# Routed experts in 256-row blocks with copied stationary weights, and the residual plus normalised x formed in place on ScalarE

## The chip, the cores and the metric

One core of a Trainium2 chip runs the kernel. The metric is the device time of one execution in microseconds (us). The engines are TensorE (PE in the profile; its weight loads are PEld), VectorE (DVE), ScalarE (ACT), GpSimd (POOL) and SyncE (SP). Each runs its own stream of instructions, and they meet only at semaphores.

## The reference

x has 8 x 1024 tokens of 256 features, so 8192 tokens. The layer is a macaron: half a feed-forward step, one attention step, half a feed-forward step, all in float32.

```python
x = x + 0.5 * ffn(layernorm(x))
x = x + attn(layernorm(x))
x = x + 0.5 * ffn(layernorm(x))

def attn(x):                       # per batch of 1024 tokens, D = 256
    q, k, v = x @ Wq.T, x @ Wk.T, x @ Wv.T
    fk = rfft(k); fk = fk / (abs(fk) + 1e-8)
    fq = rfft(q); fq = fq / (abs(fq) + 1e-8)
    return x + irfft(cumsum(fk * rfft(v), axis=-2) * conj(fq))

def ffn(x):
    shared = (silu(x @ sw1) * (x @ sw3)) @ sw2          # hidden 512
    s = sigmoid(x @ router_w.T)                         # 8 experts
    # the top 2 of s + bias, with gates s / sum(s of the two)
    routed = sum over the token's 2 experts: gate_e * (gelu(x @ ew1[e]) @ ew2[e])   # hidden 256
    return shared + routed
```

attn is given layernorm(x) and adds it once more, so the attention step yields x + layernorm(x) + values.

## The kernel before

Tokens are handled in tiles of 128 and chunks of J = 4 tiles (512 tokens, CH = 16 chunks). All of x stays in SBUF as X. Five stages follow each other: phase A and phase B of the first feed-forward, attention, phase A and phase B of the second, then a last loop that combines and stores. Within a stage every engine runs the same loop of steps (`run_steps`, L106: a few steps written out, then a hardware loop of 2 or 4 steps a turn, then the rest) in an order written by hand. No planner is involved. A step mixes work of neighbouring items, so that each engine has something to do while the others finish.

Every matmul operand is split in a high and a low part ("h" and "l", fp32r), and each product is three matmuls (`three`, L645; its lines L647 to L649 are what the profile shows). ScalarE makes the high part with a copy (L476) and VectorE the low part with a subtraction (`low`, L906, shown as L908).

Phase A computes the shared feed-forward and the router, and scatters each token's normalised row (264 floats, with the row's goal in column 256) into DRAM lists, one per expert, by GpSimd's indirect DMAs (L401). Then `block_table` (L1081) counts on one partition how many 128-row blocks each expert has, and writes a table of BLOCKS = 136 entries with the first row of each block and its expert. SP fills up the last block of each expert (eight DMAs at L322, each with a register read from the table by `value_load`).

Phase B walks over the blocks two at a time: PAIRS = 68 steps a layer. For pair s:

- SP reads two registers and loads two blocks of 128 rows into XB, a ring of 4 slots (L328). It waits for s_bl of the pair 4 before.
- PE transposes them (four 128 x 128 transposes, L783), ScalarE makes XBT high, VectorE first copies the goal column (L1128) and then makes XBT low.
- PE computes the hidden layer with the token block as stationary operand (128 x 128) and the expert's weights as moving operand, 256 columns, at an address from a register: 2 blocks x 2 k x 3 = 12 matmuls. ScalarE applies Gelu (L561), with tokens on the partitions.
- PE transposes the result (four again, L773), ScalarE makes HT high from PSUM, VectorE HT low.
- PE computes the output, again 12 matmuls of 256 columns. VectorE copies it to YB (L1134), and GpSimd scatters it to DRAM with two indirect DMAs (L412), at rows given by `goal`.

PE's order in step s (L766) is: transposes of hidden s-1, transposes of input s+1, 12 matmuls of hidden s, two register loads for s+1, 12 matmuls of output s-1. ScalarE's is HT high s-1, XBT high s+1, Gelu s. VectorE's is HT low s-1, goal and XBT low s+1, YB s-1.

In attention (16 steps) VectorE's step (L1138) adds the values of chunk s-3 to X (L1146), combines the two experts' results of chunk s+2 with X (L1155), takes its statistics (L915, L919), and then does the products of the spectra (L1170 to L1205). GpSimd's step (L423) has the sums of squares (L428), the prefix sums (L440 to L450), rstd and shift (L374, `rstd_of`), the products L456 to L462, and last X = X + XN for chunk s+1 (L466). ScalarE's step (L566) evicts PSUM, has the inverse square root by tables (L589 to L595), and makes XN = x * rstd + shift with four activations (L601), before it evicts q (L610) and the high part of the transposed XN (L614).

## Time and profile before

| | us |
|---|---|
| median of 3 runs | 1908.54 (1908.44 to 1914.2) |
| the profiled execution, its own time | 1914.37 |
| its span, first to last instruction | 1912.5 |
| PE busy | 1524.1 (80%) |
| PEld busy | 1354.9 (71%) |
| DVE busy | 1297.0 (68%) |
| ACT busy | 740.8 (39%) |
| POOL busy | 850.9 (44%) |

The profile is of one execution. The shares are means over stages with different limits, so they have to be read stage by stage. Matmuls overlap each other: the duration shown for one (some 280 ns) is longer than the distance from one to the next.

### The profile page before, as it was taken

How to read it: one execution, taken by the hardware profiler on the slowest of the kernel's cores; microseconds unless marked ns; L12 is line 12 of the kernel's file. 1: busy time of each engine (PE TensorE's matmuls, PEld its weight loads, DVE VectorE, ACT ScalarE, POOL GpSimd, SP SyncE). 2: the span in 40 equal slices, each digit the busy share in tenths (PEclk: the TensorE clock that was granted, in tenths of full speed). 3: DMA queues.
4: the chain of work that ended last, by engine and by line, in shares of the span. 5: the costliest groups of instructions: out<-in, count | busy, mean ns of one | idle time of the engine just before them, and what ended most of it. 6: DMA issues, size and time to landing. Idle time of an engine off the chain costs nothing. (4 is left out here: it accounts for less than half of the span.)

```text
span 1912.5 us, 35484 instructions
## 1 busy us (share of the span) xinstructions
PE 1524.1 (80%) x10030; PEld 1354.9 (71%) x10031; DVE 1297.0 (68%) x3148; ACT 740.8 (39%) x1161; POOL 850.9 (44%) x948
## 2 busy tenths in 40 slices
PE   2899999939999965777777874999999849999930
PEld 1777777739999965677777763777777749999930
DVE  4777888734555536899999855778887635555557
ACT  4333343314444423555555533343333224444410
POOL 1444444404444432666666642544545314444420
PEclk9999999969999986899999986999999979999975
DMA  8211111124444432111111001111111134444469
GB/s 286 88 52 51 55 47 45 57 63 127 133 134 134 128 125 66 45 44 44 44 44 44 0 1 48 55 46 45 52 50 54 49 85 133 133 134 133 131 212 348
DMA packets 123780, 170.36 MB, mean 89 GB/s; under 512 B 14880, under 2 KB 105392, under 8 KB 123440
## 3 DMA queue, kind: packets, MB, share of 16 engines
q1 hardware_dynamic: 89936, 91.05, 16.2%
q0 software_dynamic: 25344, 70.29, 10.1%
q10 hardware_dynamic: 8448, 8.39, 1.3%
q8 instruction: 25, 0.41, 0.1%
q14 instruction: 27, 0.22, 0.0%
HBM read 91.03 MB, written 81.89 MB: 90 GB/s over the span
## 5 line engine op out<-in xcount | busy, mean ns | idle before, releaser
L412 POOL DMA_INDIRECT results<-b_yb,b_goal x272 | 261.5, 961 | 368.0 <-DVE b_yb L1134 296.3
L401 POOL DMA_INDIRECT lists<-a_rows,a_slots x256 | 265.3, 1036 | 117.5 <-issue 64.5
L1134 DVE COPY b_yb<-bank 128x512 f32<-128x512 f32 x136 | 94.1, 692 | 195.8 <-PE bank L649 183.5
L647 PE MATMUL bank<-a_sw2h,a_uh 128*128 128x256 f32 x512 | 152.2, 297 | 37.5 <-DVE a_xtl L908 30.5
L476 ACT ACTIVATE a_uh<-a_gate_u 128x512 fp32r<-128x512 f32 x128 | 77.1, 624 | 255.0 <-PE bank L649 202.1
L476 ACT ACTIVATE b_hth<-bank 128x512 fp32r<-128x512 f32 x136 | 81.5, 599 | 242.9 <-PE bank L773 239.7
L647 PE MATMUL bank<-ew_h,b_hth 128*128 x544 | 162.8, 299 | 15.9 <-DVE b_htl L908 7.7
L647 PE MATMUL bank<-t_wfh,t_xah 128*128 128x256 f32 x384 | 126.2, 329 | 57.9 <-DVE t_xal L908 57.9
L647 PE MATMUL bank<-ew_h,b_xbth 128*128 x544 | 166.3, 306 | 0.6 <-DVE b_xbtl L908 0.4
L648 PE MATMUL bank<-ew_l,b_xbth 128*128 x544 | 154.8, 284 | 0.0
L649 PE MATMUL bank<-ew_h,b_xbtl 128*128 x544 | 154.6, 284 | 0.0
L649 PE MATMUL bank<-ew_h,b_htl 128*128 x544 | 153.7, 283 | 0.0
L648 PE MATMUL bank<-ew_l,b_hth 128*128 x544 | 153.6, 282 | 0.0
L648 PE MATMUL bank<-a_sw2l,a_uh 128*128 128x256 f32 x512 | 146.3, 286 | 0.0
L649 PE MATMUL bank<-a_sw2h,a_ul 128*128 128x256 f32 x512 | 146.1, 285 | 0.0
L908 DVE TENSOR_TENSOR b_htl<-bank,b_hth 128x512 fp32r<-128x512 f32 x136 | 94.1, 692 | 57.4 <-ACT b_hth L476 49.9
L647 PEld LDWEIGHTS bank<-t_wfh,t_xah 128*128 128x128 f32 x384 | 85.2, 222 | 64.5 <-DVE t_xal L908 32.1
L647 PEld LDWEIGHTS bank<-a_sw2h,a_uh 128*128 128x128 f32 x512 | 98.6, 193 | 44.2 <-DVE a_xtl L908 36.2
L783 PE MATMUL bank<-cst,b_xb 128*128 128x128 f32 x544 | 84.1, 278 | 52.9 <-DMA b_xb<-lists 27.7
L647 PEld LDWEIGHTS bank<-ew_h,b_hth 128*128 128x128 f32 x544 | 103.4, 190 | 32.0 <-issue 30.9
L396 POOL COPY a_rows<-tok 128x4 int32 (+1 forms) x64 | 12.8, 200 | 250.3 <-DVE a_slots L1024 199.3
L648 PE MATMUL bank<-t_wfl,t_xah 128*128 128x256 f32 x384 | 119.8, 312 | 0.0
(190 smaller groups left out, 4776.9 us busy)
## 6 DMA issues: line engine op xcount, KB each, us to landing
b_xb<-lists SPq DMA_DIRECT2D x272, 132.0 KB
t_yg<-results SPq DMA_DIRECT2D x32, 512.0 KB, 4.7
f_yf<-results SPq DMA_DIRECT2D x32, 512.0 KB, 10.8
X<-in_L_attn_x SPq DMA_DIRECT2D x16, 512.0 KB, 4.1
out<-X ACTq DMA_DIRECT2D x16, 512.0 KB, 7.2
results<-b_yb,b_goal POOLq DMA_INDIRECT x272
w_raw_ew<-in_L_ffn_ew SPq DMA_DIRECT2D x2, 2048.0 KB, 12.6
lists<-a_rows,a_slots POOLq DMA_INDIRECT x256
```

What stands on the lines that cost most here:

```text
L396: ch.link(pool.tensor_copy(rows[:, q, :, D:D + 1].bitcast(I32), tok[:, bass.ds(c * J + k * TILES, J)].unsqueeze(2)))
L401: pool.indirect_dma_start(out=lists, out_offset=bass.IndirectOffsetOnAxis(ap=slots[:, q, k, j:j + 1], axis=0), in_=rows[:, q, j, :], in_of ...
L412: pool.indirect_dma_start(out=results, out_offset=bass.IndirectOffsetOnAxis(ap=goal[:, slot, blk:blk + 1], axis=0), in_=YB[:, slot, blk, : ...
L476: return act.activation(o, i, ACT.Copy)
L647: pe.matmul(o, a("h"), b("h"), start=first, stop=False)
L648: pe.matmul(o, a("h"), b("l"), start=False, stop=False)
L649: return pe.matmul(o, a("l"), b("h"), start=False, stop=last)
L783: ins = pe.transpose(bank[:, 1 - par, (2 * k + blk) * P:(2 * k + blk + 1) * P], XB[:, slot, blk, k * P:(k + 1) * P], ident)
L908: return dve.tensor_tensor(o, v, h.bitcast(F32), ALU.subtract)
L1134: dve.tensor_copy(YB[:, slot].rearrange("p b d -> p (b d)"), bank[:, 7 - par, :]).then_inc(s_yok, 1)
```

## The change

A block has BR = 256 rows, and an expert's list is filled up to a multiple of 256. A step of phase B now is one block of one expert. The number of steps a layer is the most that can be needed, PAIRS = (16384 + 8 * 255) // 256 = 71. The hidden layer is computed with the weights as stationary operand, copied before by ScalarE (high) and VectorE (low) from the expert's place to a double buffer W1, and with the 256 tokens as moving operand, so that the hidden features lie on the partitions and HB needs no transpose. HT is made from HB in SBUF. `goal` is copied last in VectorE's step, with a semaphore of its own that SP waits for. In attention, GpSimd makes rstd_1 = 1 + rstd, and ScalarE forms X = X * rstd_1 + shift in place with four more activations, in place of GpSimd's addition. The diff, cut to its core:

```diff
@@ block_table: TILES -> FULL = TOKENS // BR, BLOCKS -> PAIRS, P -> BR throughout; CAP = TOKENS + BR; SPARE = E * BR
+PAIRS = (TOPK * TOKENS + E * (BR - 1)) // BR
+TURNS = [(PAIRS - i + 3) // 4 for i in range(4)]
+        HB = place("b", "hb", [P, 2, 2 * HR], F32)
+        HT = {h: place("b", f"ht{h}", [P, 2, KD, BR], F32R) for h in "hl"}
+        W1 = {h: place("b", f"w1{h}", [P, 2, KD * HR], F32R) for h in "hl"}
@@ sync
-            sp.dma_start(lists[E * CAP:E * CAP + E * P, :], fill[E * P:2 * E * P, :]).then_inc(s_spare, 16)
+            sp.dma_start(lists[E * CAP:E * CAP + SPARE, :], fill[SPARE:2 * SPARE, :]).then_inc(s_spare, 16)
-                    sp.dma_start(lists[bass.ds(end, P), :], fill[e * P:(e + 1) * P, :]).then_inc(s_tail, 16)
+                    sp.dma_start(lists[bass.ds(end, BR), :], fill[e * BR:(e + 1) * BR, :]).then_inc(s_tail, 16)
-                    atleast(sp, s_bl, n + (p0 - 3) if not isinstance(n, int) or n >= 4 else 0)
-                    for blk in range(2):
-                        row = sp.value_load(table[0:1, bass.ds(n * 2 + blk, 1)], ...)
-                        sp.dma_start(XB[:, slot, blk, :], lists[bass.ds(row, P), :]).then_inc(s_xb[slot], 16)
+                    atleast(sp, s_goal, n + (p0 - 3) if not isinstance(n, int) or n >= 4 else 0)
+                    row = sp.value_load(table[0:1, bass.ds(n, 1)], min_val=0, max_val=E * CAP + SPARE - BR)
+                    sp.dma_start(XB[:, slot, :, :],
+                                 lists[bass.ds(row, BR), :].rearrange("(b p) r -> p b r", p=P)).then_inc(s_xb[slot], 16)
@@ gpsimd
+                if residual:
+                    apart(pool)
+                    ch.link(pool.tensor_scalar(rstd_1[:, q, :], rstd[:, q, :], 1.0, 1.0, ALU.add, ALU.mult))
+                    ch.settle()
-                if nxt:
-                    pool.wait_ge(s_txn, s + 2)
-                    xc = X[:, bass.ds((s + 1) * J, J), :]
-                    pool.tensor_tensor(xc, xc, XN[:], ALU.add).then_inc(s_add, 1)
@@ scalar, phase_b
-                    if inside(s - 1, PAIRS):
-                        act.wait_ge(s_hT, s + p0)
-                        copy(HT["h"][:, 1 - par]..., bank[:, 4 + 1 - par, :]).then_inc(s_hh, 1)
                     if inside(s + 1, PAIRS):
                         ...
+                        e = act.value_load(table[0:1, bass.ds(s + (PAIRS + 1), 1)], min_val=0, max_val=E - 1)
+                        atleast(act, s_mm1, s + p0)
+                        copy(W1["h"][:, 1 - par], EW[1, "h"]...[:, bass.ds(e, 1), :]...).then_inc(s_w1h, 1)
                     if inside(s, PAIRS):
                         act.wait_ge(s_mm1, s + (p0 + 1))
+                        atleast(act, s_hl, s + (p0 - 1))
                         act.activation(HB[:, par], bank[:, 2 + par, :], ACT.Gelu).then_inc(s_gelu, 1)
+                        act.wait_ge(s_gelu, s + (p0 + 1))
+                        atleast(act, s_yps, s + (p0 - 1))
+                        copy(HT["h"][:, par].rearrange("p m t -> p (m t)"), HB[:, par]).then_inc(s_hh, 1)
@@ scalar, attention
-                    atleast(act, s_add, s + 1)
                     atleast(act, s_atp, s + 1)
                     for j in range(J):
                         ins = act.activation(XN[:, j, :], ...)
                     ins.then_inc(s_txn, 1)
+                    act.wait_ge(s_txn, s + 2)
+                    apart(act)
+                    for j in range(J):
+                        xt = X[:, bass.ds((s + 1) * J + j, 1), :].rearrange("p a d -> p (a d)")
+                        ins = act.activation(xt, xt, ACT.Identity, bias=shift[:, 1 - par, j:j + 1],
+                                             scale=rstd_1[:, 1 - par, j:j + 1])
+                    ins.then_inc(s_add, 1)
@@ tensor, phase_b
-                    for blk in range(2):
-                        pe.reg_load(offset[par][blk], table[0:1, bass.ds(s * 2 + (BLOCKS + blk), 1)])
+                    pe.reg_load(offset[par], table[0:1, bass.ds(s + PAIRS, 1)])
-                    if inside(s - 1, PAIRS):
-                        pe.wait_ge(s_gelu, s + p0)
-                        ...                      # the transposes of HB, L771 to L775
+                        pe.wait_ge(s_w1h, s + (p0 + 1))
+                        pe.wait_ge(s_w1l, s + (p0 + 1))
                         atleast(pe, s_gelu, s + (p0 - 1))
-                        for blk in range(2):
+                        for m in range(KD):
                             for k in range(KD):
-                                ins = three(bank[:, 2 + par, blk * HR:(blk + 1) * HR],
-                                            lambda h: XBT[h][:, par, k, blk, :],
-                                            lambda h: expert(1, h, at[blk], k), k == 0, k == KD - 1)
+                                ins = three(bank[:, 2 + par, m * BR:(m + 1) * BR],
+                                            lambda h: W1[h][:, par, k * HR + m * P:k * HR + (m + 1) * P],
+                                            lambda h: XBT[h][:, par, k].rearrange("p b t -> p (b t)"),
+                                            k == 0, k == KD - 1)
@@ vector, phase_b, the whole step after
+                    if inside(s + 1, PAIRS):
+                        dve.wait_ge(s_bh, s + (p0 + 2))
+                        low(XBT["l"][:, 1 - par]...).then_inc(s_bl, 1)
+                        e = dve.value_load(table[0:1, bass.ds(s + (PAIRS + 1), 1)], min_val=0, max_val=E - 1)
+                        atleast(dve, s_mm1, s + p0)
+                        dve.tensor_copy(W1["l"][:, 1 - par], EW[1, "l"]...[:, bass.ds(e, 1), :]...).then_inc(s_w1l, 1)
+                    if inside(s, PAIRS):
+                        dve.wait_ge(s_hh, s + (p0 + 1))
+                        low(HT["l"][:, par]..., HB[:, par], HT["h"][:, par]...).then_inc(s_hl, 1)
+                    if inside(s - 1, PAIRS):
+                        dve.wait_ge(s_yps, s + p0)
+                        dve.tensor_copy(YB[:, slot]..., bank[:, 7 - par, :]).then_inc(s_yok, 1)
+                    if inside(s + 1, PAIRS):
+                        atleast(dve, s_ysc[slot], turn * 32 + YW[slot] * layer)
+                        dve.tensor_copy(goal[:, slot, :], XB[:, slot, :, D].bitcast(I32)).then_inc(s_goal, 1)
```

The loops of phase B end three steps earlier (`PAIRS - 3`), and three steps are written out behind them, because 71 is no multiple of 4.

## Rows read from the trace of the kernel before

**Rows 1.** Phase B, attention: window, length, busy PE, PEld, DVE, ACT, POOL, clock, DMA.
```profile
421.00:705.00 284.00, 269.78 (x2176) 260.72 (x2176) 142.46 (x272) 116.13 (x205) 130.72 (x136) 0.98 0.42 126
723.00:1112.00 389.00, 292.75 (x1814) 272.38 (x1815) 341.74 (x478) 214.70 (x237) 242.00 (x212) 0.89 0.13 41
```
**Rows 2.** PE timeline, first and last input transposes of a phase B (start, us).
```profile
421.40 1.09 PE L783 MATMUL bank<-cst,b_xb 128*128 128x128 f32 x4 [25.72 <-DMA b_xb<-lists]
...
690.47 0.60 PE L783 MATMUL bank<-cst,b_xb 128*128 128x128 f32 x4
...
1556.46 1.08 PE L783 MATMUL bank<-cst,b_xb 128*128 128x128 f32 x4 [25.18 <-issue]
...
1823.54 0.60 PE L783 MATMUL bank<-cst,b_xb 128*128 128x128 f32 x4
```
**Rows 3.** PE timeline, one step of phase B and the next one's transposes.
```profile
541.81 0.60 PE L773 MATMUL bank<-cst,b_hb 128*128 128x128 f32 x4
542.25 0.60 PE L783 MATMUL bank<-cst,b_xb 128*128 128x128 f32 x4
...
545.56 0.60 PE L773 MATMUL bank<-cst,b_hb 128*128 128x128 f32 x4
```
**Rows 4.** ACT and DVE groups over the whole kernel: count, busy, mean ns, idle before.
```profile
L908 DVE TENSOR_TENSOR b_htl<-bank,b_hth 128x512 fp32r<-128x512 f32 x136 | 94.1, 692 | 57.4 <-ACT b_hth L476 49.9
L1128 DVE COPY b_goal<-b_xb x136: 157/169/410, 423.2 to 1825.2; 128x2 int32<-128x2 int32 x136
L476 ACT ACTIVATE a_uh<-a_gate_u 128x512 fp32r<-128x512 f32 x128 | 77.1, 624 | 255.0 <-PE bank L649 202.1
```
**Rows 5.** POOL timeline, the first scatter of two consecutive steps of phase B.
```profile
455.74 0.96 POOL L412 DMA_INDIRECT results<-b_yb,b_goal  x1 [2.10 <-DVE b_yb L1134]
...
459.02 0.96 POOL L412 DMA_INDIRECT results<-b_yb,b_goal  x1 [1.06 <-issue]
```
**Rows 6.** SP timeline: issues without and with a register read.
```profile
706.97 0.46 SPq L345 DMA_DIRECT2D t_raw_w<-in_L_attn_Wv  x1
...
405.31 10.09 SPq L322 DMA_DIRECT2D lists<-in_c_fill  x8
...
9.55 5.52 SPq L309 DMA_DIRECT2D lists<-in_c_fill  x1
```
**Rows 7.** DVE timeline: the largest operation of the block table, the first statistics.
```profile
400.83 2.41 DVE L1103 TENSOR_REDUCE b_line<-b_past 1x272 f32<-1x2176 f32 x1
...
26.59 1.41 DVE L915 BATCH_NORM_STATS2 st<-X 128x6 f32<-128x256 f32 x4 [0.18 <-DVE carry L1077]
```
**Rows 8.** DVE timeline, one step of attention.
```profile
952.78 1.21 DVE L908 TENSOR_TENSOR t_xal<-bank,t_xah 128x1024 fp32r<-128x1024 f32 x1
956.41 1.60 DVE L1203 TENSOR_TENSOR t_kv<-t_kv 128x508 f32<-128x508 f32 x1
958.05 0.69 DVE L1205 TENSOR_TENSOR t_kv<-t_ta,t_tb 128x508 f32<-128x508 f32 x1
967.82 0.66 DVE L1170 TENSOR_TENSOR t_ta<-bank,t_fq 128x508 f32<-128x508 f32 x1
976.85 1.21 DVE L908 TENSOR_TENSOR t_xal<-bank,t_xah 128x1024 fp32r<-128x1024 f32 x1
...
L1170 DVE TENSOR_TENSOR t_ta<-bank,t_fq 128x508 f32<-128x508 f32 x16 | 10.7, 668 | 31.5 <-PE bank L865 31.5
```
**Rows 9.** POOL, PE and ACT timelines of the same step.
```profile
953.86 2.38 POOL L466 TENSOR_TENSOR X<-X,t_xn 128x1024 f32 x1
956.20 1.26 POOL L428 TENSOR_TENSOR t_sq<-t_sq 128x508 f32<-128x508 f32 x1
...
966.64 0.59 PE L865 MATMUL bank<-t_px,cst 128*128 128x256 f32 x2
...
967.41 2.08 ACT L601 ACTIVATE t_xn<-X,shift,rstd 128x256 f32 x4
971.07 1.02 ACT L476 ACTIVATE t_xah<-bank 128x1024 fp32r<-128x1024 f32 x1
```

More of the change, by code:

```diff
@@ L160, in build @@
         shift = sb("shift", [P, 2, J], F32)
+        rstd_1 = sb("rstd_1", [P, 2, J], F32)
         neg_one = sb("neg_one", [P, J], F32)
@@ L805, in step @@
                         for blk in range(2):
-                            for k in range(KD):
+                            for m in range(KD):
                                 ins = three(bank[:, 7 - par, blk * D:(blk + 1) * D],
-                                            lambda h: HT[h][:, 1 - par, k, blk, :],
-                                            lambda h: expert(2, h, at[blk], k), k == 0, k == KD - 1)
+                                            lambda h: HT[h][:, 1 - par, m, blk * P:(blk + 1) * P],
+                                            lambda h: expert(2, h, before, m * HR, HR), m == 0, m == KD - 1)
                         ins.then_inc(s_yps, 1)
                 pe.wait_ge(s_table, layer + 1)
-                offset = [[pe.alloc_register(f"expert_{layer}_{par}_{blk}") for blk in range(2)] for par in range(2)]
-                run_steps(pe, step, -1, 4, PAIRS - 4, PAIRS + 1, 4)
+                offset = [pe.alloc_register(f"expert_{layer}_{par}") for par in range(2)]
+                run_steps(pe, step, -1, 4, PAIRS - 3, PAIRS + 1, 4)
             def attention_weights():
@@ L1114, in phase_b @@
                 p0 = PAIRS * layer
+                dve.wait_ge(s_table, layer + 1)
                 def step(s, u, q):
```

118 lines of the change are left out of this document (52 added, 66 removed).

## The prediction, made before the changed kernel was run

> **What bounds the kernel now.** I read the page's slices first, then the busy time by stage, then the timelines of the stages that the diff touches. A share of the span would mislead: phase B and attention have different limits. In phase B PE is busy 269.78 of 284 us at a clock of 0.98, its weight loads 260.72, while DVE has 142.46, ACT 116.13 and POOL 130.72 [rows 1]. In attention DVE has 341.74 of 389 us and PE 292.75 [rows 1], most of DVE's idle time lying at the stage's two ends and in a few waits for PE.
>
> Phase B's pace is the distance from one step's input transposes to the next one's. From the first to the last of 68 steps are 690.47 - 421.40 = 269.1 us, over 67 intervals 4.02 us; in the second layer 1823.54 - 1556.46 = 267.1 us, 3.99 us [rows 2]. A step in which nothing stalls takes 545.56 - 541.81 = 3.75 us [rows 3]. So PE's own work makes 3.75 us, and stalls make some 0.26 us in the mean.
>
> **Phase B, PE.** The four transposes of the hidden tile go. Four transposes take 542.25 - 541.81 = 0.44 us of PE [rows 3]. Both kernels have 24 matmuls of 256 columns and 4 input transposes beside them. Stationary and moving operand change places in 12 matmuls, for which I take no price: one 128-column load and one 256-column matmul stay one of each. PE's work for a step becomes 3.75 - 0.44 = 3.31 us. One of two register loads a step goes as well. The steps rise from 68 to 71, intervals from 67 to 70, since all 71 are computed whatever the counts are. At 3.31 us they take 231.7 us; at the old mean 4.02 they would take 281.4. The stalls of 0.26 us should shrink. Before, the stalled instruction is mostly the second product, waiting for HT low, whose chain starts with PE's transposes only one product ahead (transpose, ScalarE, VectorE, 1.45 us, of which 0.6 + 0.69 are the two engines [rows 4]). After, the chain is Gelu, HT high, HT low, 0.6 + 0.62 + 0.69 = 1.9 us with some 0.3 us of handing over, 2.2 us, and it has an output product, a set of transposes and a hidden product to hide in, 1.43 + 0.44 + 1.43 = 3.3 us (a product of 12 matmuls being half of what 3.75 - 2 x 0.44 leaves). I leave a third of the stalls, 0.09 us: 3.40 us a step, 70 x 3.40 = 238.0 us. That is -31.1 us in the first layer and -29.1 in the second.
>
> **Phase B, the others, against 3.40 us.** ScalarE gains the copy to W1 high. Its nearest row is the copy between two SBUF tiles of the same size, 0.624 us [rows 4]. Four of them are 2.5 us, and a register read is added. VectorE has XBT low, W1 low, HT low, YB, goal: 0.69 for each of the first four at most, the subtraction HT low being 0.692 [rows 4] and 0.17 for the last, 2.9 us. The copy W1 low shows in no row: it lies between 0.16 us (the smallest goal copy) and 0.69 us (the subtraction of the same size); I take 0.69 as the nearest in size. What the register read costs shows on SP only: an issue takes 0.46 us without one, and 10.09 / 8 = 1.26 us with one, so up to 0.8 us [rows 6]. I count it as hidden on both engines, because it runs in the sequencer while the copy before it (0.6 to 0.69 us) is still at work; if it isn't hidden, VectorE needs 2.9 + 0.8 = 3.7 us, and this is a rival. POOL's least distance between the first scatters of two steps is 459.02 - 455.74 = 3.28 us, where the idle time is put to issue, not to DVE [rows 5]. So POOL can just follow a PE at 3.31. SP has one read and one DMA of twice the rows instead of two of each: less. The ring of four slots is freed later in the step (goal is now last), which leaves some two and a half steps, 8.5 us, for one issue and one transfer of 264 KB, at a DMA share of 0.42 now [rows 1].
>
> The Trainium skill has a rule against this change. "SBUF — State Buffer", section "Who interferes with whom", says that a VectorE copy between SBUF tiles in a two-port mode and a GpSimd instruction exclude each other for their whole length, and that GpSimd's descriptor generation needs that port. What the rows show is the goal copy, between 157 and 410 ns with a median of 169 [rows 4], so a copy was held by 0.24 us at most. By the rule in full, a scatter and W1 low would wait for each other up to 0.96 us a step. The rule's own result, as a mechanism of this kernel, is the second rival.
>
> **Around phase B.** The block table has 71 entries instead of 136 and 32 thresholds instead of 64. Its largest reduction falls from 2.41 us [rows 7] to some 1.3, and the operations ahead of it, which are shorter and shrink alike, by 2.2 us together: -3.3 us a layer. The eight fills carry twice the rows. One fill of 1024 rows is issued in 5.52 us, 5.4 ns a row [rows 6]; 128 rows more are +0.7 us if that holds for them, and nothing if the issue has a fixed price as the loads of 256 rows with 0.46 us suggest. The eight lie between 0 and +5.5; I take +2.8. The first hidden product waits for W1 too, +0.5 us. The sum is 0 a layer, between -3 and +3. At the start SP issues a fill of 2048 rows before the loads of X: +5.5 us for the X loads. The first statistics start at 26.59 with no wait for X [rows 7], so part of it is hidden behind expert weights: +2 us, between 0 and +5.
>
> **Attention.** GpSimd's addition of 2.38 us goes [rows 9]. DVE's L1203 took 1.60 us, and L1205, of the same size and also on SBUF tiles, 0.69 [rows 8]; L1203 ran against GpSimd's L428 (956.20 to 957.46 [rows 9]). With the addition gone, L428 follows 2.38 us earlier, beside products that read PSUM and are not slowed. So DVE gets back 1.60 - 0.69 = 0.9 us a step. What is late next is PE: L1170 needs the prefix sums' last matmul, which starts at 966.64 and ends at 967.1 to 967.2, and L1170 ran at 967.82 [rows 8, 9]. So 0.65 to 0.73 us can be kept. Nine of the steps are of this kind; in the others L1170 waits for PE already (31.5 us in 16 [rows 8]) and nothing is gained. 9 x 0.7 = -6.5 us, between -14 (0.9 us in all 16) and 0. ScalarE's four more activations cost 2.08 us like those of L601 [rows 9]. They stand ahead of q's eviction and of XA high, which then starts at 973.2 instead of 971.07 [rows 9] and ends at 974.2; the subtraction that waits for it starts at 976.85 (a period of 24.07 after 952.78 [rows 8]), and at 976.1 with the gain. Thus they are covered by 1.8 us, and would cost 2.1 us x 16 = 33 us if that cover were gone. GpSimd's rstd_1 comes before s_rstd, a small operation that I put at 0.3 us (the goal copy's 0.17 [rows 4] with a wait behind it); GpSimd is idle 147 of 389 us [rows 1], and what it takes is lost in that.
>
> **The sum** against the profiled execution, 1914.37 us: -31.1 - 29.1 - 6.5 + 0 + 2 = -64.7, so 1849.7 us. That execution is 5.8 us above the median of 1908.54; with the same difference off, 1843.9: I say 1844 us.
>
> **Rivals.**
> - Register reads on the path, VectorE as the bound. For it: VectorE's 2.9 us is the second longest sum, and its order makes every step wait for ScalarE twice. Against it: PE reads two registers a step now, and still has steps of 3.75 us without a gap. At 3.7 us a step, 70 x 3.7 = 259.0: -10.1 - 8.1, and 1914.4 - 18.2 - 6.5 + 2 - 5.8 = 1886 us.
> - The copy and the scatters exclude each other, by 0.33 us a step (half of 0.69, the copy in a mode twice as fast, holding GpSimd once). GpSimd's 3.28 becomes 3.61 us, 252.7 us a layer: -16.4 - 14.4, 1873 us.
> - The slow side: GpSimd is held by a copy of full length, 3.28 + 0.69 = 3.97 us. 70 x 3.97 = 277.9: +8.8 + 10.8, 1914.4 + 19.6 - 6.5 + 2 - 5.8 = 1924 us. It decides from 269.1 / 70 = 3.84 us a step on. For it: GpSimd's floor is so near PE's. Against it: the goal copies, always beside scatters, have a median of 169 ns.
> - Attention turns the other way, ScalarE's activations delaying XA high: up to +33 us, with the gain of phase B left 1883 us. Against it stands ScalarE's idle time, 174 of 389 us [rows 1], 10.9 us a step.
>
> **How the numbers follow.** The forecast has a chance of 0.63, the first rival 0.12, the second 0.11, attention 0.03, the slow one 0.06, and 0.05 is left for a phase B with no stall at all (3.31: 70 x 3.31 = 231.7, -6.3 twice more) together with attention at its best, 1844 - 12.6 - 7.5 = 1824 us. The range is 1822 to 1882: below it nearly nothing, above it the first rival's greater part and the slow one. From 1908.54, 0.3% is 5.7 us, about what a measurement of this kernel can tell from no change. Faster by more has 0.90, within it 0.03, slower by more 0.07.
>
> **What would show it.** Right: in phase B the distance of input transposes near 3.4 us with PE (PEld too) the busiest engine, 71 of them; L1203 at 0.69; DVE still without gaps in attention, period 23.4. Wrong: W1 low followed by idle time of PE on it (first rival); scatters longer than 0.96 us or idle time of POOL's put to a DVE copy, W1 low longer than 0.69 (second and slow rival); t_xal waiting for ACT (attention). The prediction falls if a step of phase B takes more than 3.6 us.

## The result, and the profile after

| group of runs | before, us | after, us | ratio, 95% interval | phase B of after, first and second layer |
|---|---|---|---|---|
| first (the prediction's) | 1908.35 | 1922.89 | 1.0058, 1.0039 to 1.0077 | 271.2, 269.6 |
| c_after, chip 2 | 1910.08 | 1916.40 | 1.0015, 0.9976 to 1.0054 | 274.0, 274.2 |
| z_after, chip 6 | 1876.81 | 1823.30 | 0.9715, 0.9699 to 0.9732 | 231.5, 231.3 |

Forecast were 1844 us and a range of 1822 to 1882: the measured result, 1922.89, lies outside and on the slow side. The later groups show that the sign hangs on the chip, or on its state at the time. Where before takes 1908 to 1910 us (the first group's chip and chip 2; on chip 4, with before at 1908.58, only variants of after ran) the change gives nothing or costs 0.6%; where before takes 1877 (chip 6; on chip 3 again only variants) it gives 53.5 us. Chips 2 and 4 served one group of runs each, so a lasting property of a chip can't be told from a state that it was in. Ratios leave the slow executions out: 1940.72 us among the 20 of after, 3081.38 among the 11 of e_attn, 2595.1 among the three of before beside e_noscatter.

Phase B is one profiled execution's, from the start of the first input transpose to the start of the very last one. That is 0.3 us more than the starts in [rows 2] give; before's two layers, counted so, are 269.4 and 267.4 us.

The two profiled executions of after, the first group's (own time 1905.47, span 1903.6, the fastest of its 20 and 17 us under their median; where the median execution lost those 17 us no trace shows) and z_after's (span 1821.6), have the same instructions. First the windows of [rows 1] (phase B and attention, the same columns), in the first group's:

```profile
421.00:705.00 284.00, 248.11 (x1988) 241.42 (x1986) 168.64 (x355) 170.13 (x285) 143.79 (x141) 0.97 0.44 131
723.00:1112.00 389.00, 295.06 (x1836) 274.46 (x1837) 331.19 (x481) 246.48 (x302) 211.26 (x214) 0.89 0.13 41
```

PE's busy time in phase B has fallen from 269.78 us to 248.11, the part of the forecast that came true; but the window is still filled: 36 us of PE's time are gaps now, against 14. The page's groups (whole kernel; count, busy, mean ns, idle time before and what ended it) say at which instruction:

```profile
L911 DVE TENSOR_TENSOR b_htl<-b_hb,b_hth 128x512 fp32r<-128x512 f32 x142 | 98.3, 692 | 185.8 <-ACT b_hth L480 147.8
L661 PE MATMUL bank<-ew_h,b_hth 128*128 x568 | 166.9, 294 | 56.2 <-DVE b_htl L911 55.5
L661 PE MATMUL bank<-b_xbth,b_w1h 128*128 128x256 f32 x568 | 175.0, 308 | 3.5 <-DVE b_w1l L1130 2.2
L566 ACT ACTIVATE b_hb<-bank 128x512 f32<-128x512 f32 x142 | 83.9, 591 | 112.1 <-remote 86.4
```

PE waits for HT low (55.5 us in both layers), hardly for W1 low (2.2), and Gelu, L566, waits 86.4 us with "remote" as releaser: the profile finds no end of an instruction near the moment at which the wait ended. The same two products in z_after have no such wait:

```profile
L661 PE MATMUL bank<-b_xbth,b_w1h 128*128 128x256 f32 x568 | 173.6, 306 | 3.0 <-DVE b_w1l L1130 3.0
L661 PE MATMUL bank<-ew_h,b_hth 128*128 x568 | 159.5, 281 | 1.5 <-DVE b_htl L911 1.5
```

One slow step out of the first group's trace, PE's transposes, the hidden product's last matmul, Gelu and what follows (start, duration, in brackets the idle time before and its releaser):

```profile
509.23 0.28 PE L663 MATMUL bank<-b_xbth,b_w1l 128*128 128x256 f32 x1
...
510.77 0.60 PE L786 MATMUL bank<-cst,b_xb 128*128 128x128 f32 x4
...
511.60 0.60 ACT L566 ACTIVATE b_hb<-bank 128x512 f32<-128x512 f32 x1 [2.12 <-remote]
512.23 0.63 ACT L480 ACTIVATE b_hth<-b_hb 128x512 fp32r<-128x512 f32 x1
512.89 0.69 DVE L911 TENSOR_TENSOR b_htl<-b_hb,b_hth 128x512 fp32r<-128x512 f32 x1 [2.62 <-ACT b_hth L480]
...
513.82 0.38 PE L661 MATMUL bank<-ew_h,b_hth 128*128 x1 [1.02 <-DVE b_htl L911]
...
515.34 0.60 PE L786 MATMUL bank<-cst,b_xb 128*128 128x128 f32 x4
```

The hidden product's last matmul ends at 509.23 + 0.28 = 509.51. Gelu needs nothing else and sits idle, yet starts at 511.60: PE's release comes 2.1 us after the matmul's modelled end. From there the chain takes just the 2.2 us that the prediction gave it (511.60 to 513.82), but with 2.1 + 2.2 = 4.3 us in front of a cover of 3.3, PE stands idle for 1.02 us, and the step lasts 515.34 - 510.77 = 4.57 us. The step before it took 3.29. So phase B alternates over long stretches: of 70 steps of the first layer some 40 take 3.28 to 3.4 us, 22 take 4.3 to 5.5, two 7.0 and 8.5. In z_after 66 of 70 take 3.28 or 3.29 us, and Gelu starts when the product ends:

```profile
505.45 0.60 ACT L566 ACTIVATE b_hb<-bank 128x512 f32<-128x512 f32 x1
...
506.67 0.60 PE L786 MATMUL bank<-cst,b_xb 128*128 128x128 f32 x4
506.75 0.69 DVE L911 TENSOR_TENSOR b_htl<-b_hb,b_hth 128x512 fp32r<-128x512 f32 x1 [0.81 <-ACT b_hth L480]
...
509.95 0.60 PE L786 MATMUL bank<-cst,b_xb 128*128 128x128 f32 x4
```

How late a release is, is read as the moment at which PE raises the semaphore less the modelled end of the matmul that carries it. In the first group's trace of after it is over 1 us for the hidden product in 36 of the 132 steps whose release is on record, mostly 2.0 to 2.8 (and 0.4 to 0.6 in the step between two such), 1.7 to 1.9 us for the input transposes in some 45 steps and 2.1 to 2.3 for the output product in some 42; the late ones of one stretch come together (513.15, 513.21, 513.34). The kernel before shows the same thing smaller, mostly 0.4 to 0.6 us behind its HT transposes and up to 0.8 behind the output product. In z_after none is over 0.1 us.

Two things go with it. Late releases aren't confined to phase B: in phase A of the first trace of before the release of the shared output product is late by up to 1.3 us, in after's by up to 1.4, in z_after never. And the traces with late releases lack records of semaphores: of 143 rises behind the hidden product after has 136, of 143 behind the output product 127, before 91 of 137 behind the hidden product, though the matmuls' own records are all there; no trace without late releases lacks more than one of such a semaphore. Each timed execution has its span and clock from the profiler, so whether releases come late without the recording no run shows.

### The profile page after: what moved, and what is told of

It reads as the page before. It is cut to its first block and busy times, and to the rows that moved or that the text cites. A ratio compares the mean times of both kernels' runs of the same rounds, so it can differ in the third digit from the quotient of the medians.

```text
span 1903.6 us, 34118 instructions
## 1 busy us (share of the span) xinstructions
PE 1481.1 (78%) x9654; PEld 1318.8 (69%) x9655; DVE 1330.2 (70%) x3315; ACT 878.2 (46%) x1386; POOL 839.8 (44%) x960
## 5 line engine op out<-in xcount | busy, mean ns | idle before, releaser
L420 POOL DMA_INDIRECT results<-b_yb,b_goal x284 | 290.7, 1023 | 336.2 <-DVE b_yb L1139 237.0
L911 DVE TENSOR_TENSOR b_htl<-b_hb,b_hth 128x512 fp32r<-128x512 f32 x142 | 98.3, 692 | 185.8 <-ACT b_hth L480 147.8
L661 PE MATMUL bank<-ew_h,b_hth 128*128 x568 | 166.9, 294 | 56.2 <-DVE b_htl L911 55.5
L661 PE MATMUL bank<-b_xbth,b_w1h 128*128 128x256 f32 x568 | 175.0, 308 | 3.5 <-DVE b_w1l L1130 2.2
L661 PE MATMUL bank<-a_sw2h,a_uh 128*128 128x256 f32 x512 | 151.9, 297 | 23.2 <-DVE a_xtl L911 16.1
L662 PE MATMUL bank<-ew_l,b_hth 128*128 x568 | 163.6, 288 | 0.0
L662 PE MATMUL bank<-b_xbtl,b_w1h 128*128 128x256 f32 x568 | 162.3, 286 | 0.0
L663 PE MATMUL bank<-b_xbth,b_w1l 128*128 128x256 f32 x568 | 161.9, 285 | 0.0
L661 PEld LDWEIGHTS bank<-ew_h,b_hth 128*128 128x128 f32 x568 | 110.3, 194 | 64.7 <-issue 64.7
L480 ACT ACTIVATE b_xbth<-bank 128x512 fp32r<-128x512 f32 x142 | 84.5, 595 | 141.3 <-PE bank L786 125.5
L566 ACT ACTIVATE b_hb<-bank 128x512 f32<-128x512 f32 x142 | 83.9, 591 | 112.1 <-remote 86.4
L496 ACT ACTIVATE a_gate_u<-bank 128x512 f32<-128x512 f32 x128 | 75.4, 589 | 128.2 <-PE bank L663 63.9
L911 DVE TENSOR_TENSOR b_xbtl<-bank,b_xbth 128x512 fp32r<-128x512 f32 x142 | 97.5, 687 | 47.9 <-ACT b_xbth L480 45.0
```

What stands on the lines that cost most here:

```text
L420: pool.indirect_dma_start(out=results, out_offset=bass.IndirectOffsetOnAxis(ap=goal[:, slot, blk:blk + 1], axis=0), in_=YB[:, slot, blk, : ...
L480: return act.activation(o, i, ACT.Copy)
L496: act.activation(gate_u[:, m % 2, :], bank[:, 2 + 2 * (m % 2), :], ACT.Sigmoid).then_inc(s_sig, 1)
L566: act.activation(HB[:, par], bank[:, 2 + par, :], ACT.Gelu).then_inc(s_gelu, 1)
L661: pe.matmul(o, a("h"), b("h"), start=first, stop=False)
L662: pe.matmul(o, a("h"), b("l"), start=False, stop=False)
```

## Experiments

Theory at the start: PE's releases come late by 2 us whatever the kernel does, and the cover is too short for that. Rivals: the W1 copies or register reads disturb PE or the chain; PE's own work is what is late.

### One part alone, more cover, fewer suspects (chip 3)

e_attn is the kernel before with the attention part alone:

```
-                    pool.tensor_tensor(xc, xc, XN[:], ALU.add).then_inc(s_add, 1)
+                        ins = act.activation(xt, xt, ACT.Identity, bias=shift[:, 1 - par, j:j + 1],
+                                             scale=rstd_1[:, 1 - par, j:j + 1])
```

> The kernel before with the attention part alone (blocks of 128 rows as before; rstd_1, the residual in place on ScalarE, GpSimd's addition gone). Theory: the two parts are independent and phase B is where the forecast failed. Then this gives what the attention stage showed in the trace after, 423.4 - 419.5 = 3.9 us, so 1904 to 1905 against 1908.5, with the stage near 419.5 us and phase B unchanged at 269 and 267 us. Rival: the stage gained 3.9 us only in the one profiled execution, and ScalarE's four activations more cost as much as GpSimd's addition: 1908 to 1909. Second rival: ScalarE delays XA high in most steps, 1915 or more.

Measured: 1881.56 against 1877.21, ratio 1.0021 (1.0012 to 1.0031). The part alone doesn't gain, it costs 4 us. Its attention stage, from VectorE's first combination (L1155) to the last matmul of the values, takes 423.1 us. It is 423.4 in the first trace of before, and between 417.6 and 424.2 in the kernels with blocks of 256, whose attention is e_attn's, so a gain of the part isn't clear of the scatter between traces; its phases B take 253.8 and 255.2 us, though their code is that of before (269.4, 267.4). None of its releases is late. The clue to all that follows is in the other column: before itself measured 31 us less here.

e_deep puts the output product two steps behind the hidden one:

```
-                        pe.wait_ge(s_hl, s + p0)
+                        pe.wait_ge(s_hl, s + (p0 - 1))
-                                             lambda h: HT[h][:, 1 - par, m, ...
+                                             lambda h: HT[h][:, (u + 2) % 4, m, ...
```

> The kernel after, with PE's output product two steps behind the hidden product instead of one (four buffers of HT and four expert registers for two, eight rows of goal for four, VectorE waits for the scatter's landing before it fills YB). The chain from the hidden product over Gelu, HT high and HT low has then two whole PE steps, 6.6 us, to hide in, instead of 3.3. Theory: the long steps come from releases by PE that arrive up to 2.0 to 2.8 us after the last matmul's modelled end, so that a chain of 2.2 us becomes 4.3 to 5.0 us against a cover of 3.3. With 6.6 us it is covered: a step of phase B near 3.3 to 3.4 us, 70 x 3.35 = 234.5 instead of 271.2 and 269.6, 72 us less than after: 1835 to 1855 us. Rival: PE's own work is what is late, so the releases tell the truth and the recorded starts run ahead of the work; then PE needs some 3.8 us a step whatever the cover is, and the time stays at 1900 to 1925.

e_nocopy:

```
-                        copy(W1["h"][:, 1 - par], EW[1, "h"] ... [:, bass.ds(e, 1), :] ...
-                                             lambda h: W1[h][:, par, k * HR + m * P: ...
+                                             lambda h: EW[1, h][:, k * HR + m * P: ...
```

> The kernel after without the W1 copies on ScalarE and VectorE and without their register reads; PE takes the stationary weights of the first product straight from expert 0 for every block, so the choice of the expert for the first product is left out. Theory (late releases by PE in front of too short a cover): the releases stay late by some 2 us, since PE's instructions are the same; Gelu alone starts a little earlier in the steps where W1 high stood ahead of it (0.64 us), so a step of 3.7 to 3.87 us, 1895 to 1922. Rival (the copies and register reads are what disturbs the chain or PE's reads of SBUF): the late releases go with the copies, 3.3 to 3.4 us a step, 1835 to 1855.

e_peconst:

```
-                        before = weights_at(1 - par)
-                        load_expert(s + 1, 1 - par)
+                        before = 0
```

> The kernel after with expert 0's weights for every block's output product at a fixed address: PE loads no register between the hidden and the output product and addresses no weights by one (the choice of the expert for the second product is left out). Theory (late releases have to do with PE running without a break, not with registers): no change, step 3.8 to 3.9 us, 1905 to 1930. Rival (the register load or the address from it delays PE's releases): the hidden product's release comes 0 to 0.1 us after its end again, 3.3 to 3.4 us a step, 1835 to 1860.

Measured beside 1877.21: e_deep 1829.37 (0.9748), e_nocopy 1821.08 (0.9702), e_peconst 1828.30 (0.9738), phases B 229.7, 228.0 and 231.4 us. They lie within 8 us of one another, and no release is late in any: the group couldn't tell the theories apart, since the thing to be explained wasn't there. After itself did not run in it.

### The same on a chip where it is (chip 2)

> The kernel after once more, unchanged, with the kernel before beside it on the same chip. In the last group of runs the kernel before itself was 31 us faster than in the group in which after was first measured (1877.2 against 1908.4), its phase B stepped at 3.71 us in the median against 4.03, and no release by PE came late. Theory: the late releases are a property of the chip (or its state), not of a kernel, and they decide what the change is worth. Where before measures 1877, after has steps near 3.3 us and 1828 to 1845; where before measures 1908, after is at 1905 to 1940 again. Rival: the late releases belong to this kernel (its PE has no break in which they could catch up), so it is at 1900 or more on every chip.

> The kernel with the output product two steps behind, once more, beside after on the same chip. Theory: with a cover of 6.6 us it steps at 3.3 us wherever it runs. On a chip where releases are late it is 60 to 80 us ahead of after; where they are in time, after has the same steps and the two differ by under 10 us. Rival (PE's own work lags where releases are late): there it gains under 20 us over after.

> The kernel without the W1 copies and their register reads once more, beside after on the same chip. Theory: the copies cost nothing where releases are in time (within 12 us of after, the 5 us at the phases' ends and 0.03 us a step included), and where releases are late they don't cause it: releases of the hidden product still 2 us late in part of the steps, over 3.6 us a step. Rival: the copies disturb PE, late releases vanish here alone, 3.3 us a step.

> The kernel with a fixed address and no register load on PE once more, beside after on the same chip. Theory: within 6 us of after where releases are in time; where they are late, late here too and within 15 us of after. Rival (register load delays PE's releases): 3.3 us a step here, 60 us or more ahead of after, wherever it runs.

| beside before at 1910.08 | us | phase B, both layers | us a step |
|---|---|---|---|
| c_after | 1916.40 | 274.0, 274.2 | 3.91 |
| c_deep | 1898.82 | 267.1, 260.2 | 3.82, 3.72 |
| c_peconst | 1872.41 | 245.6, 246.6 | 3.51, 3.52 |
| c_nocopy | 1840.43 | 237.8, 238.3 | 3.40 |

The first theory falls with c_deep: twice the cover buys 18 us of the 93 between c_after and z_after, which is inside what was written down for the rival, that PE's own work lags (under 20). Its waits in phase B (engine, line, what it waited for: total us, times, longest) show that the wait has moved to the next hand-off from PE, the one over the input transposes and the W1 buffers:

```profile
PE bank L662 <- DVE b_w1l L1132: 28.7, 25, 2.1
ACT b_hb L567 <- PE bank L664: 28.7, 31, 3.4
ACT b_hb L567 <- remote: 27.2, 9, 3.8
PEld bank L662 <- DVE b_xbtl L912: 27.0, 20, 2.1
```

That the copies and the register load are innocent falls too: without the copies 76 us go, without PE's load 44. So each adds to the trouble; how, this doesn't show. A fuller PE isn't what adds: c_nocopy has the shortest steps of the four and, on record, the fewest releases over 1 us late (36, against 132 in c_after).

### Splitting the copies from the reads, and two ways around (chip 4)

e_noread keeps the W1 copies at a fixed address; e_noregs also takes PE's load away. e_selfwait and e_deeper:

```
+                    if inside(s, PAIRS):
+                        pe.wait_ge(s_mm1, s + (p0 + 1))
```
```
-                    if inside(s + 1, PAIRS):
-                        atleast(pe, s_bl, s + p0)
+                    if inside(s + 2, PAIRS):
+                        atleast(pe, s_bl, s + (p0 - 1))
```

> The kernel after with the W1 copies kept but taken from expert 0 at a fixed address, so that ScalarE and VectorE read no register (the choice of the expert for the first product is left out; PE still loads its register). It splits what the kernel without the copies took away: 1840 us against 1916 for after on the same chip. Theory A (register reads make PE's releases late): near 1845 us where before measures 1908. Theory B (the copies' traffic in SBUF does it): near 1900 to 1920 there. Where before measures 1877, 1825 to 1840 by both.

> The same, and PE too works from expert 0 at a fixed address without a register load; only SyncE still reads one (the choice of experts is left out of both products). By theory A no release by PE comes late any more, 3.3 us a step and 1825 to 1840 us where before measures 1908. By theory B the copies still disturb: 1860 to 1900 there, as the kernel with PE's load alone taken away (1872). Where before measures 1877, 1825 to 1835 by both.

> The kernel after with one wait more: PE waits for its own release of the hidden product before it begins the output product. Theory C (a release is done in time but isn't delivered while PE's instructions follow each other without a break): the pause delivers it at once, each step costs some 0.25 us more than 3.29 and no long steps are left: 3.55 us a step, 248 us a phase, some 1875 us where before measures 1908. Theory D (the release itself is 2 us late, or the product truly ends so late): PE now waits 2 us in every second step, 4.3 us a step, 1960 us or more there. Where before measures 1877 both give some 1860 us.

> The kernel with the output product two steps behind, and now the input transposes and the W1 copies a step earlier as well (four buffers of XBT and W1, two more PSUM banks for the transposes). In the first of these, on the chip with late releases, PE no longer waited for HT low but for XBT low (27 us) and W1 low (29 us) of a phase. Theory: each hand-off from PE has now at least 4.9 us for a chain of 1.3 to 2.2 us, so a release 2 us late is covered: 3.3 to 3.4 us a step and 1825 to 1845 us on every chip. Rival (PE's own work is slower there than its recorded starts): 3.7 us a step and more, 1890 us or more where before measures 1908.

| beside before at 1908.58 | us | ratio, 95% interval | phase B, both layers |
|---|---|---|---|
| e_noread | 1900.89 | 0.9956, 0.9928 to 0.9985 | 263.8, 280.4 |
| e_noregs | 1874.95 | 0.9802, 0.9773 to 0.9832 | 250.3, 252.6 |
| e_selfwait | 1893.84 | 0.9906, 0.9882 to 0.9931 | 265.2, 265.5 |
| e_deeper | 1907.96 | 0.9986, 0.9964 to 1.0008 | 266.3, 261.1 |

Taking ScalarE's and VectorE's reads away gives 15 to 22 us against the 1916 and 1923 of after (other groups and chips), not the some 70 of theory A, which fails for them; with PE's load gone as well it is 1875, what c_peconst had by that alone. What c_nocopy gained beyond would lie in the copies themselves (theory B), but the two were on different chips. e_deeper refutes the first theory again, and shows what a late stretch looks like from inside:

```profile
566.70 0.28 PE L664 MATMUL bank<-b_xbtl,b_w1h 128*128 128x256 f32 x1 [0.48 <-issue]
567.45 0.28 PE L664 MATMUL bank<-b_xbtl,b_w1h 128*128 128x256 f32 x1 [0.23 <-issue]
568.17 0.38 PE L665 MATMUL bank<-b_xbth,b_w1l 128*128 128x256 f32 x1 [0.44 <-issue]
568.23 0.60 ACT L568 ACTIVATE b_hb<-bank 128x512 f32<-128x512 f32 x1 [4.43 <-remote]
```

PE itself comes to a halt in the middle of a product, with "issue" as the reason, nothing that it waits for. The hidden product that ended at 563.52 by its modelled end was released at 568.21, then the output product and the transposes behind it at 568.34 and 568.39, where by their own length they would have needed 1.4 and 0.4 us more. So they were done, and were held up behind the first. That is against theory D (work that truly ends late, all of it), though the time of e_deeper is the one written down for it. The run e_selfwait speaks for theory C: the hidden product is released at once in all but 5 of the 108 steps on record, and the long steps are nearly gone. Of its 140 steps 96 take 3.69 to 3.71 us, among them those in which nothing is late (546.23 to 549.92), so the pause itself seems to cost 0.4 us a step where 0.25 was expected; 28 take 3.79. The run wasn't made where no release is late, so that price isn't measured apart. Late in part are still the output product and the transposes, mostly by 0.3 to 0.8 us, here by 1.0:

```profile
572.18 0.60 PE L786 MATMUL bank<-cst,b_xb 128*128 128x128 f32 x4
...
573.85 0.60 ACT L480 ACTIVATE b_xbth<-bank 128x512 fp32r<-128x512 f32 x1 [1.80 <-PE bank L786]
```

In e_deeper's late stretches the scatters' queue moves 109 GB/s and that of the XB loads 91, outside them 25 and 50 (in c_after 106 and 101 against 51 and 59). That made the transfers the next suspect (theory E), although a late stretch and a busy queue may only fall into the same part of a step.

### Transfers left out (chips 3 and 6)

e_noscatter, e_noload and e_quiet leave transfers out of the second layer's phase B, with the first layer as control:

```
+                    if layer == 1:
+                        pool.sem_inc(s_skip[slot], 32)
+                        return
```
```
+                    if layer == 1 and not isinstance(n, int):
+                        sp.sem_inc(s_xb[slot], 16)
+                        return
```

> The kernel after with GpSimd's scatters left out in the second layer's phase B alone (GpSimd only raises the semaphores that VectorE and SyncE wait for; the second layer's expert results are not written), the first layer's phase B as it is, so that one trace holds the case and its control. Where the first layer shows long steps (3.8 to 3.9 us in the mean), theory E (transfers in or out of SBUF hold back PE's completions; in the traces so far the queues move 106 and 101 GB/s in the stretches with a late release and 51 and 59 outside) has the second layer at 3.3 to 3.6 us a step. Theory F (the cause lies between the engines, in the copies or register reads): the second layer stays at 3.8 to 3.9 us. On a chip without late releases both layers step at 3.3 us and nothing is told apart.

> The same with the loads of XB left out in the second layer's phase B, apart from its first four and last three blocks (SyncE only raises the semaphore; PE works on old tokens). Theory E: the second layer's steps are shorter than the first layer's by 0.2 us or more, more than without the scatters if writes into SBUF are what holds PE back. Theory F: the same steps in both layers.

> Both the loads of XB and the scatters left out in the second layer's phase B. Theory E: no release comes late in the second layer, 3.3 us a step there against 3.8 to 3.9 in the first, and 38 us less in all than after. Theory F: 3.8 to 3.9 us in both layers, under 8 us less than after.

> The kernel without XB loads and scatters in the second layer's phase B once more, since in the last group before measured 1877 to 1883 and no release came late in either layer (3.30 and 3.29 us a step). Where before measures 1908 and the first layer shows 3.8 to 3.9 us a step: theory E has 3.3 us in the second layer and no release late by more than 0.1 us; theory F has 3.8 to 3.9 in both.

> The kernel without XB loads and scatters in the second layer's phase B, beside after. Where before measures 1908: theory E has 3.3 us a step in the second layer against 3.8 to 3.9 in the first, theory F 3.8 to 3.9 in both. Where before measures 1880 it is within 8 us of after and tells nothing of the cause.

All five runs fell on chips 3 and 6, where no release is late: 1821.38, 1825.92 and 1823.80 us beside before at 1880.2 (two executions, 1877.04 and 1883.36), 1822.33 beside 1882.42, 1814.65 beside 1876.81, with 231.3 to 231.6 us in the first layer and 230.6 to 230.9 in the second. Whether transfers hold the releases back stays open. What they do show: here the transfers cost phase B under 1 us in 231, and the control layers are five more traces of after at 3.31 us a step.

### After on a chip without late releases

> The kernel after, unchanged, for its own ratio in one group of runs with the kernel before. Theory (the chip decides): where before measures 1877 to 1883, after is at 1820 to 1832, 0.973 of it, with 3.30 us a step, as the first layers of the last four kernels showed; where before measures 1908, after is at 1905 to 1930. Rival (the changes to the second layer made the last kernels' times): over 1840 where before measures 1880.

Measured: 1823.30 against 1876.81, ratio 0.9715 (0.9699 to 0.9732), 3.31 and 3.30 us a step. The chip, or its state, decides, as the theory said. Its phase B and attention, in the windows of [rows 1]:

```profile
421.00:705.00 284.00, 255.12 (x2084) 252.50 (x2084) 187.67 (x407) 184.94 (x303) 165.61 (x158) 0.94 0.50 149
723.00:1112.00 389.00, 292.17 (x1770) 267.56 (x1770) 320.59 (x435) 234.58 (x284) 213.78 (x206) 0.90 0.12 37
```

(Phase B's last matmul ends at 657.4 in this trace and its last scatter at 661.8, so the first window holds the head of attention too.)

No version is shown to be the best everywhere. Where releases come late, e_selfwait (0.9906) and c_deep (0.9945) are ahead of before, and after is not; where they come in time, after is (0.9715, and e_deep 0.9748 on another chip). Of e_selfwait there is no run there.

## Why the prediction was wrong

**PE's own step.** Right: 3.28 to 3.29 us measured where nothing stalls, 3.31 forecast; the exchange of stationary and moving operand costs nothing, and the steps are 71.

**The stalls.** This is the step that failed: "The stalls of 0.26 us should shrink ... I leave a third ... 0.09 us: 3.40 us a step". Measured 3.87 and 3.85, stalls of 0.58 us; with 70 intervals 271.2 and 269.6 us in place of 238.0 and 238.0. And that is the fastest of the 20 executions. The working read the stalls of before as a chain with too little cover. The trace of before had the contrary in it. In the step of [rows 3] whose transposes start at 545.56 and end 0.60 later, at 546.16, the chain goes on thus:

```profile
546.72 0.60 ACT L476 ACTIVATE b_hth<-bank 128x512 fp32r<-128x512 f32 x1 [1.80 <-PE bank L773]
547.35 0.69 DVE L908 TENSOR_TENSOR b_htl<-bank,b_hth 128x512 fp32r<-128x512 f32 x1 [0.74 <-ACT b_hth L476]
...
548.18 0.38 PE L647 MATMUL bank<-ew_h,b_hth 128*128 x1 [0.16 <-DVE b_htl L908]
```

ScalarE had been idle for 1.80 us and starts 0.56 us after the end that it waits for; it starts 0.4 us or more behind in 28 of the 59 steps between 430 and 670 us, and 0.04 us behind in 23. The forecast rested on durations added up, without a look at the gaps between an end and the start that it releases. Those gaps are no constant of handing over; they grow with the new kernel to over 2 us, and belong to PE's side. e_attn, with the old phase B, takes 253.8 us where they are absent: 3.79 a step, near the bare 3.75. In after they made the chain of 2.2 us one of 4.3, longer than its cover of 3.3. A longer cover alone didn't mend it (c_deep, e_deeper), so the chain is only where the late release first shows.

**The falling point.** "The prediction falls if a step of phase B takes more than 3.6 us": it does, and the slow rival's point, 3.84 us, is passed, but by another mechanism than any named. That its 1924 us lies 1 us from the measured time is chance: GpSimd, its bound, is idle 336.2 us before its scatters. GpSimd's "floor" of 3.28 us is none either: in z_after two first scatters lie 535.13 - 531.98 = 3.15 us apart.

**The copies and register reads.** Their direct costs were right or too high: W1 high 0.64 us; W1 low 0.41 to 0.46 in z_after, not 0.69. VectorE as the bound (first rival) didn't come, 168.64 of 284 us busy. ScalarE's register read isn't always hidden, as it was taken to be: in z_after it sits idle for 0.15 to 0.45 us before W1 high in 113 of 142 steps, with "issue" as the reason, which its slack takes up.

The second rival has a true core, but not the one named. A scatter takes 1118 ns in the mean in z_after and 959 in e_attn, 0.32 us more a step on GpSimd, and the 0.33 of the rival is near it by chance: in e_nocopy, which has no W1 copy at all, it is 1131. The diff brought two VectorE instructions with all their tiles in SBUF, W1 low and also HT low, which before took one input from PSUM. A scatter is longer when one of them is already at work as it starts. In z_after scatters that start during W1 low take 1142 ns in the mean (103 of them), during HT low 1208 (106), all others 959 (75), and a step's second scatter starts later by what the first takes more; in e_nocopy it is 1326 during HT low and 959 else; in e_attn, where HT low reads PSUM, 958 and 959. One pair from e_nocopy:

```profile
530.08 0.69 DVE L905 TENSOR_TENSOR b_htl<-b_hb,b_hth 128x512 fp32r<-128x512 f32 x1 [1.37 <-ACT b_hth L480]
530.13 1.47 POOL L420 DMA_INDIRECT results<-b_yb,b_goal  x1 [0.30 <-issue]
```

and three scatters from z_after:

```profile
531.98 1.07 POOL L420 DMA_INDIRECT results<-b_yb,b_goal  x1 [1.18 <-DVE b_yb L1139]
533.03 0.69 DVE L911 TENSOR_TENSOR b_htl<-b_hb,b_hth 128x512 fp32r<-128x512 f32 x1 [0.81 <-ACT b_hth L480]
533.35 1.20 POOL L420 DMA_INDIRECT results<-b_yb,b_goal  x1 [0.30 <-issue]
...
535.06 0.43 DVE L1130 CAST b_w1l<-ew_l 128x512 fp32r x1
535.13 1.19 POOL L420 DMA_INDIRECT results<-b_yb,b_goal  x1 [0.58 <-issue]
```

For W1 low the traces bear out one side of the rule in the Trainium skill, "SBUF — State Buffer", section "Who interferes with whom", that whoever issues first holds the shared port and the other waits: a copy that starts first lengthens the scatter, by up to 0.25 us. The other side they don't: the 31 W1 low that start inside a scatter in the first group's trace of after take 0.46 us in the mean, against 0.42 for the rest, and none more than 0.67.

It costs no time, because GpSimd has 3.30 - 2 x 1.118 = 1.06 us of slack a step. Where releases come late the copies go with up to 76 us (chip 2); no term or rival had that.

**Around phase B.** Right within its bounds: from PE's last work of phase A to the second layer's first transposes 23.2 us against 25.2, so -2 a layer (0 forecast, -3 to +3); phase A of the first layer ends 1.9 us later (forecast +2).

**Attention.** Half right, and the gain isn't shown. The stage takes 419.5 us against 423.4, -3.9 instead of -6.5, but e_attn has the same attention and 423.1. L1213, which was L1203, takes 0.69 us as forecast, and L1165, the combination, no longer than before (eight take 5.55 us here and 5.82 there). Rows of DVE in one step of before and one of after:

```profile
959.85 4.15 DVE L1155 SCALAR_TENSOR_TENSOR X<-t_yg,gates,X 128x256 f32 x4
964.15 1.67 DVE L1155 SCALAR_TENSOR_TENSOR X<-t_yg,gates,X 128x256 f32 x4 [0.15 <-DVE X L1155]
```

```profile
949.69 1.21 DVE L911 TENSOR_TENSOR t_xal<-bank,t_xah 128x1024 fp32r<-128x1024 f32 x1
953.32 0.69 DVE L1213 TENSOR_TENSOR t_kv<-t_kv 128x508 f32<-128x508 f32 x1
955.85 3.18 DVE L1165 SCALAR_TENSOR_TENSOR X<-t_yg,gates,X 128x256 f32 x4
959.18 2.37 DVE L1165 SCALAR_TENSOR_TENSOR X<-t_yg,gates,X 128x256 f32 x4 [0.15 <-DVE X L1165]
964.04 0.69 DVE L1180 TENSOR_TENSOR t_ta<-bank,t_fq 128x508 f32<-128x508 f32 x1 [0.41 <-PE bank L868]
973.12 1.21 DVE L911 TENSOR_TENSOR t_xal<-bank,t_xah 128x1024 fp32r<-128x1024 f32 x1
```

The period is 23.43 us here, the 23.4 forecast, but 24.38 in every other step (mean of all 15 periods 23.79, against 23.93 before). VectorE now waits for PE before L1180 in nearly every step: 0.41 us in the short ones and 1.24 in the long ones, where [rows 8] have no wait before L1170. So the time given back by L1203 was kept in one step and lost to PE in the next; what makes PE 0.8 us later in the long steps isn't shown. The forecast gave all nine steps the gain of the one that it had read. ScalarE's activations delayed nothing, as forecast. That the part alone costs 4 us in e_attn isn't explained; there is no trace of before on that chip to set beside it.

**The sum where releases are in time.** Against e_attn's phases B, z_after's are -22.3 and -23.9 us; with -2 x 2 around them, some -3 in attention (419.8 against 423.1) and +2 at the start that makes -51, and -53.5 was measured. The attention term is borrowed: both of these traces have the new attention, and before has no trace on such a chip. The forecast had -64.7, from a baseline that held 12 to 16 us a layer of late releases. Its absolute figure, 1844, would have been 21 us too high there.

**What stays open.** What holds PE's releases back, why on some chips and not on others, and how the copies and the register load add to it. Shown is that a longer cover alone doesn't mend it, and that it shrinks when the copies or PE's register load are taken away or PE is made to pause. The transfers were left out only on chips where nothing was late, and no run was made without the recording, whose records go missing in just these traces.

## What to carry over

Before stalls are booked as missing cover, look at each gap between a producer's end and the start that it alone releases; a gap in which the waiting engine is idle and the producer has ended is a late release, and here it hit the tighter kernel harder (stalls of 0.58 us a step in place of 0.26). This change was worth 3% on one chip and nothing on another: time before and after together on more than one chip before the change is judged. Where the releases themselves are late, giving one hand-off more room moved the wait to the next (c_deep). And a contention that one run puts down to a new instruction wants the run without that instruction: the scatters stay long without the W1 copy.

## What was not expected of the hardware

- The same program takes 1908 or 1877 us by the chip, with the mean granted clock of the whole span the same (0.915 and 0.917 for after), the same median packet times in the queues (159 ns for the scatters, 47 for the loads), and the same attention stage (420.3 and 419.8 us). Of the 96 us between c_after and z_after 85 lie in the two phases B.
- A matmul's semaphore can rise 4.7 us after its modelled end (563.52 to 568.21, e_deeper), and releases behind it then come within 0.2 us.
- The traces with late releases lack records of semaphores (c_peconst has 92 of 143 behind the output product), the others at most one of each behind PE's products.
- A VectorE instruction with all tiles in SBUF that is at work when a scatter starts lengthens it, from 0.96 us to 1.2 and up to 1.47; with one input in PSUM it doesn't (e_attn).
- PE can stand still inside a product on such a chip, with no wait recorded.
- A register read takes 0.26 to 0.30 us in the median in the sequencers of SyncE, ScalarE, VectorE and PE. In z_after VectorE's was hidden behind the instruction before it in all but 3 of 142 steps, ScalarE's in only 29.
